# Perceiver block on one core: the opening loads of the context regrouped, the first batch's Gram sums in banks of their own, a new order of steps, and a shorter close

## What is computed

```python
# cross attention, 16 heads, no softmax: x = x + this(layernorm(x), ctx_1024, ctx_1024)
score = jnp.einsum('bhqd,bhkd->bhqk', Q, K) / dk
attn = jnp.where(mask, -jnp.inf, score)
ctx = jnp.einsum('bhqk,bhkd->bhqd', attn, V)
x = residual + _linear(ctx, wo_w, wo_b)          # then layer norm with ln_g, ln_b
# self attention, 64 tokens a batch, softmax: x = x + this(layernorm(x))
attn = jax.nn.softmax(scores, axis=-1)
# second self attention with rotary q and k, then the dense part: x = x + this(layernorm(x))
x = _rmsnorm(src + sa, norm1_w)
shared = _swiglu(flat @ W_shared_in) @ W_shared_out
h = _swiglu(flat @ W1_shared)
for e in range(E):                               # w: top 2 of the best group's 4 experts
    routed = routed + h @ W2_experts[e] * w[:, e:e + 1]
return _rmsnorm(x + shared + routed, norm2_w)
```

## Time and profile before

| | us |
|---|---|
| median of 3 runs (lowest, highest) | 263.49 (262.86, 266.23) |
| the profiled execution's own time | 262.64 |
| its span, first to last instruction | 260.5 |
| TensorE busy | 240.4 (92%) |
| VectorE busy | 174.3 (67%) |
| ScalarE busy | 121.0 (46%) |
| GpSimd busy | 75.9 (29%) |
| mean DMA rate | 101 GB/s |

### The profile page before, as it was taken

The page is one execution under the profiler, slowest core; times in us unless marked ns, Lnnn a source line. Parts: engine busy times, 40 slices in busy tenths (PEclk is TensorE's granted clock), DMA queues, the critical chain, the costliest instruction groups (busy, mean ns, idle before and its releaser), DMA issues.

```text
span 260.5 us, 5316 instructions
## 1 busy us (share of the span) xinstructions
PE 240.4 (92%) x2116; PEld 213.6 (82%) x2116; DVE 174.3 (67%) x366; ACT 121.0 (46%) x240; POOL 75.9 (29%) x87
## 2 busy tenths in 40 slices
PE   8678899999999999999998899999989999999980
PEld 8677899889988899997977789888768889988860
DVE  2537857797967787976855779656699652375345
ACT  4524752391443864667253495844661435530000
POOL 2001304372224303412334237467700011520003
PEclk9799999999999999999999999999999999999996
DMA  6997769566035034065202003150000000000002
GB/s 199 381 389 262 264 201 310 179 186 230 0 93 164 0 101 153 3 177 159 80 3 84 0 1 103 60 135 32 0 0 3 0 3 3 0 0 0 3 1 81
DMA packets 8856, 26.33 MB, mean 101 GB/s; under 512 B 1400, under 2 KB 3072, under 8 KB 8576
## 3 DMA queue, kind: packets, MB, share of 16 engines
q1 hardware_dynamic: 8832, 25.99, 30.6%
HBM read 25.46 MB, written 0.52 MB: 100 GB/s over the span
## 4 chain that ended last, share of the span: by engine, by line
PE 73%; DVE 9%; issue 5%; DMA 4%; ACT 3%; POOL 3%; SPq 1%; DVEq 0%; POOLq 0%; ACTq 0%
PE ps L677 68%; PE ps L680 5%; DMA raw<-in_ctx 4%; POOL rstd L441 2%; DVE qs L1221 1%; POOL dense L476 1%; DVE Z L1013 1%; ACT ch L552 1%; DVE st L990 1%; DVE Z L1262 1%; ACT kblk L501 1%; DVE X L1271 1%; SPq L383 1%; DVE Z L1001 1%; DVE cl L1110 0%
## 5 line engine op out<-in xcount | busy, mean ns | idle before, releaser
L677 PE MATMUL ps<-ch 128*128 128x130 f32 (+1 forms) x208 | 53.0, 271 | 3.8 <-DVE cl L1110 2.3
L677 PE MATMUL ps<-ch,cl 128*128 128x260 f32 (+1 forms) x208 | 53.4, 319 | 0.0
L677 PE MATMUL ps<-w,hT 128*128 128x512 f32 x192 | 46.5, 399 | 0.0
L441 POOL TENSOR_TENSOR rstd<-ve,half_exp 128x1 f32<-128x1 f32 (+1 forms) x22 | 13.6, 622 | 112.3 <-DVE ve L985 112.2
L677 PEld LDWEIGHTS ps<-ch 128*128 128x128 f32 (+1 forms) x208 | 41.6, 200 | 4.7 <-issue 2.8
L677 PEld LDWEIGHTS ps<-w,hT 128*128 128x128 f32 x192 | 35.7, 188 | 8.8 <-issue 0.3
L677 PEld LDWEIGHTS ps<-ch,cl 128*128 128x128 f32 (+1 forms) x208 | 41.3, 198 | 0.1
L1110 DVE TENSOR_TENSOR cl<-raw,ch 128x1024 fp32r<-128x1024 f32 (+1 forms) x23 | 32.9, 1433 | 10.5 <-ACT ch L552 9.8
L552 ACT ACTIVATE ch<-raw 128x1024 fp32r<-128x1024 f32 (+1 forms) x23 | 25.8, 1132 | 7.3 <-DMA raw<-in_ctx 6.8
L677 PE MATMUL ps<-xHL,dense 128*128 128x256 f32 x192 | 23.8, 284 | 0.0
L677 PEld LDWEIGHTS ps<-xHL,dense 128*128 128x128 f32 x192 | 23.1, 189 | 0.2
(11 more groups left out here) (161 smaller groups left out, 436.4 us busy)
## 6 DMA issues: line engine op xcount, KB each, us to landing
raw<-in_ctx SPq DMA_DIRECT2D x23, 512.0 KB, 4.8
raw<-in_w SPq DMA_DIRECT2D x8, 512.0 KB, 3.7
w<-in_w SPq DMA_DIRECT2D x2, 1024.0 KB, 7.1
stage<-in_dense SPq DMA_DIRECT2D x4, 512.0 KB, 5.3
mask<-in_mask SPq DMA_DIRECT2D x1, 800.5 KB, 10.4
rows<-in_rows SPq DMA_DIRECT2D x1, 768.0 KB, 7.8
raw<-in_ctx SPq DMA_DIRECT2D x8, 65.0 KB
raw<-in_ctx SPq DMA_DIRECT2D x4, 128.0 KB, 2.4
```

The source lines that it names most:

```text
L441: pool.tensor_tensor(rstd[:, lo:hi], ve[:, lo:hi], half_exp[:, lo:hi], ALU.pow).then_inc(sem("rstd"), 1)
L677: return pe.matmul(o, l, r, start=start, stop=stop, skip_group_check=not check)
```

## The change

- **Loads of chunks 0 and 1.** Chunk 0 is loaded as row 0 and rows 1 to 3 (it was four single rows) and still split row by row; chunk 1 is loaded and split in two halves (it was whole). `gram` 1 waits for each half.
- **Loads beside.** `w0` moves from after chunk 3 to after chunk 5, `rows` from after chunk 4 to after chunk 5, the mask from after chunk 6 to after chunk 7.
- **Banks.** Batch 0's sums go to `CROSS_B` (6, 7); batch 1 starts in `GRAM_B` with no wait for `g`.
- **Order.** All four parts of the list are new. The batches' norms, the attention steps, the dense products and the weight pieces stand in other places; `last_square` and `last_root` of tiles 0 and 1 and `finish` of tiles 0 to 2 stand before the last expert steps.
- **Close.** `last_root` multiplies Z by the weight row while POOL makes the root, and `finish` is one instruction. The last expert product is made as two halves of 256 columns in two banks.

```diff
-        ("gram", 0), ("gram", 1), ("gram", 2), ("split", 0), ("split", 1), ("split", 2), ("split", 3), ("split", 4),
-        ("norm0", 0), ("evac", 0), ("gram", 3), ("norm0_end", 0), ("gram", 4), ("cross1", 0), ("split", 5),
-        ("pre", 0), ("cross2_product", 0), ("qb", 0), ("flag", 0), ("norm0", 1), ("cross2", 0), ("gram", 5),
-        ("norm0_end", 1), ("split", 6), ("split", 7), ("evac", 1), ("cross3", 0), ("pre", 1), ("cross4", 0),
-        ("cross1", 1), ("gram", 6), ("split", 8), ("cross2_product", 1), ("split", 9), ("qb", 1), ("cross2", 1),
-        ("flags", 0), ("cross3", 1), ("masked", 0), ("gram", 7), ("cross4", 1), ("split", 10), ("gram", 8),
-        ("evac", 2),
+        ("split", 0), ("gram", 0), ("gram", 1), ("gram", 2), ("split", 1), ("split", 2), ("split", 3), ("split", 4),
+        ("norm0", 0), ("evac", 0), ("gram", 3), ("split", 5), ("norm0_end", 0), ("gram", 4), ("cross1", 0),
+        ("gram", 5), ("cross2_product", 0), ("evac", 1), ("split", 6), ("cross2", 0), ("pre", 0), ("cross3", 0),
+        ("cross4", 0), ("qb", 0), ("flag", 0), ("cross1", 1), ("gram", 6), ("split", 7), ("cross2_product", 1),
+        ("split", 8), ("cross2", 1), ("gram", 7), ("norm0", 1), ("gram", 8), ("split", 9), ("norm0_end", 1),
+        ("split", 10), ("cross3", 1), ("evac", 2), ("pre", 1), ("cross4", 1), ("cross1", 2), ("qb", 1), ("flags", 0),
+        ("masked", 0),
...
-        ("xo_product", 0), ("xo", 0), ("xo_end", 0), ("norm1", 0), ("norm1_end", 0), ("split", 11), ("cross1", 2),
-        ("gram", 9), ("gram", 10), ("turn_z", (0, 0)), ("proj1_product", 0), ("piece", 0), ("split", 12),
...
+        ("xo_product", 0), ("xo", 0), ("split", 11), ("gram", 9), ("xo_end", 0), ("cross2_product", 2), ("norm1", 0),
+        ("gram", 10), ("norm1_end", 0), ("split", 12), ("gram", 11), ("cross2", 2), ("turn_z", (0, 0)), ("split", 13),
...
-        ("cross2_product", 3), ("cross2", 3), ("split", 14), ("turn_p", (0, 0)), ("cross3", 3), ("values", (0, 0)),
-        ("cross4", 3), ("project", (0, 0)), ("norm2", 0), ("norm2_end", 0), ("xo_product", 1), ("xo", 1),
-        ("gram", 14), ("split", 15), ("xo_end", 1), ("split", 16), ("turn_z", (0, 1)), ("proj2_product", 0),
-        ("evac", 4), ("rotate", 0), ("keys2", 0), ("gram", 15), ("values2", 0), ("roped", 0),
+        ("turn_p", (0, 0)), ("cross3", 3), ("split", 15), ("values", (0, 0)), ("cross4", 3), ("project", (0, 0)),
+        ("gram", 14), ("norm2", 0), ("split", 16), ("evac", 4), ("xo_product", 1), ("norm2_end", 0), ("xo", 1),
+        ("split", 17), ("xo_end", 1), ("turn_z", (0, 1)), ("gram", 15),
...
-        ("norm1", 1), ("keys_roped", 0), ("cross1", 4), ("gram", 16), ("score_product", (0, 1)), ("norm1_end", 1),
-        ("piece", 2), ("turn_z", (1, 0)), ("score", (0, 1)), ("proj1_product", 1), ("split", 17), ("queries", 1),
...
+        ("norm1", 1), ("split", 18), ("proj2_product", 0), ("gram", 16), ("rotate", 0), ("keys2", 0), ("values2", 0),
+        ("roped", 0), ("keys_roped", 0), ("norm1_end", 1), ("gram", 17), ("cross1", 4), ("turn_z", (1, 0)),
+        ("score_product", (0, 1)), ("proj1_product", 1), ("score", (0, 1)), ("piece", 2), ("piece", 3), ("split", 19),
...
+        ("xo_product", 3), ("score", (2, 0)), ("piece", 6), ("piece", 7), ("exp", (2, 0)), ("hidden_product", 0),
+        ("hidden_product", 1), ("xo", 3), ("hidden", 0), ("hidden", 1), ("hidden_product", 2), ("hidden_product", 3),
+        ("shares", (2, 0)), ("hidden", 2), ("xo_end", 3), ("hidden_product", 4), ("hidden_product", 5),
+        ("turn_p", (2, 0)), ("norm1", 3), ("norm1_end", 3), ("piece", 8), ("gates", 0), ("hidden_product", 6),
...
-        ("experts_product", (3, 3)), ("experts", (3, 1)), ("experts", (3, 2)), ("last_square", 2),
-        ("experts", (3, 3)), ("last_root", 0), ("last_root", 1), ("last_square", 3), ("last_root", 2),
-        ("last_root", 3), ("finish", 0), ("finish", 1), ("finish", 2), ("finish", 3),
+        ("hidden_product", 8), ("experts", (1, 1)), ("experts", (1, 2)), ("last_root", 0), ("experts", (1, 3)),
+        ("hidden_product", 9), ("hidden_product", 10), ("hidden", 8), ("hidden_product", 11), ("hidden", 9),
...
+        ("last_root", 2), ("experts", (3, 1)), ("finish", 1), ("experts_product", (3, 3)), ("experts", (3, 2)),
+        ("experts", (3, 3)), ("last_square", 3), ("finish", 2), ("last_root", 3), ("finish", 3),
...
+    def expert_parts(use):
+
+        return [slice(0, D), slice(D, 2 * D)] if use == HALVES * USES - 1 else [slice(0, 2 * D)]
...
-        return [(r, r + 1) for r in range(ROWS)] if n == 0 else [(0, ROWS)]
+        return ([(r, r + 1) for r in range(ROWS)], [(0, 2), (2, ROWS)])[n] if n < 2 else [(0, ROWS)]
 
     def splits(n):
 
-        return ROWS + n
+        return ROWS + n + (n > 0)
+
+    def first_loads(eng, parts, n):
+
+        src = d_ctx[0, 0:CH_B * ROWS * P, :].rearrange("(p r) d -> p r d", r=CH_B * ROWS)
+        for lo, hi in parts:
+            eng.dma_start(raw[:, ROWS * n + lo:ROWS * n + hi, :],
+                          src[:, n * ROWS + lo:n * ROWS + hi, :]).then_inc(sem(f"first{n}{lo}"), 16)
...
-                3: [(w0[:, :, :, :], d_w0, "w0_in")],
-                4: [(X[:, :, :], d_x, "x_in"), (cols[:, :], d_cols, "cols_in"),
-                    (rows[:, :, :], d_rows.partition_broadcast(P), "rows_in")],
-                6: [(mask[:, :], d_mask, "mask_in")],
+                4: [(X[:, :, :], d_x, "x_in"), (cols[:, :], d_cols, "cols_in")],
+                5: [(w0[:, :, :, :], d_w0, "w0_in"), (rows[:, :, :], d_rows.partition_broadcast(P), "rows_in")],
+                7: [(mask[:, :], d_mask, "mask_in")],
...
-                for lo, hi in chunk_parts(n):
-                    sp.dma_start(raw[:, ROWS * c + lo:ROWS * c + hi, :],
-                                 src[:, c * ROWS + lo:c * ROWS + hi, :]).then_inc(sem(f"raw{c}" if n else f"first{lo}"), 16)
+                if n == 0:
+                    first_loads(sp, [(0, 1), (1, ROWS)], 0)
+                elif n == 1:
+                    first_loads(sp, chunk_parts(1), 1)
+                else:
+                    sp.dma_start(raw[:, ROWS * c:ROWS * c + ROWS, :],
+                                 src[:, c * ROWS:c * ROWS + ROWS, :]).then_inc(sem(f"raw{c}"), 16)
...
+                    banks = GRAM_B if i else CROSS_B
                     act.wait_ge(sem("gram_chunk"), CH_B * (i + 1))
                     if i >= 2:
                         act.wait_ge(sem("gs"), i - 1)
-                    copy(gab[:, i % 2, :, :, :].rearrange("p k c n -> p k (c n)"), ps[:, GRAM_B[0]:GRAM_B[1] + 1, 0:3 * GBLK], sem("g"))
+                    copy(gab[:, i % 2, :, :, :].rearrange("p k c n -> p k (c n)"), ps[:, banks[0]:banks[1] + 1, 0:3 * GBLK], sem("g"))
...
-                    if i:
+                    if i > 1:
                         pe.wait_ge(sem("high_done"), splits(i))
                         pe.wait_ge(sem("low_done"), splits(i))
-                    if b and c == 0:
+                    banks = GRAM_B if b else CROSS_B
+                    if b > 1 and c == 0:
                         pe.wait_ge(sem("g"), b)
                     for r in range(ROWS):
                         if i == 0:
                             pe.wait_ge(sem("high_done"), r + 1)
                             pe.wait_ge(sem("low_done"), r + 1)
-                        last = gram_tile(c, r, P, c == 0 and r == 0, False)
+                        elif i == 1 and r % 2 == 0:
+                            pe.wait_ge(sem("high_done"), ROWS + r // 2 + 1)
+                            pe.wait_ge(sem("low_done"), ROWS + r // 2 + 1)
+                        last = gram_tile(banks, c, r, P, c == 0 and r == 0, False)
                     if c == CH_B - 1:
-                        last = gram_tile(c, ROWS, TAIL, False, True)
+                        last = gram_tile(banks, c, ROWS, TAIL, False, True)
                     last.then_inc(sem("gram_chunk"), 1)
...
-                    split_products(
-                        ps[:, DENSE_B[use % 4], :],
-                        [([hT[:, 1, a, k, tok] for a in range(2)], [w2[:, u, a, k, :] for a in range(2)])
-                         for k in range(HID // P)]).then_inc(sem("products"), 1)
+                    for n, cols_ in enumerate(expert_parts(use)):
+                        if n:
+                            pe.wait_ge(sem("taken"), use - 2)
+                        split_products(
+                            ps[:, DENSE_B[(use + n) % 4], cols_],
+                            [([hT[:, 1, a, k, tok] for a in range(2)], [w2[:, u, a, k, cols_] for a in range(2)])
+                             for k in range(HID // P)]).then_inc(sem("products"), 1)
...
+                    if step == "last_root":
+                        link(dve.tensor_tensor(Z[:, i, :], Z[:, i, :], rows[:, 5, :], ALU.mult))
...
-                    link(rms_scaled(5, i, root_of["last_root", i]))
```

(4 more changed lines are left out.)

114 lines of the change are left out of this document (55 added, 59 removed), and 9 rows, old and new, of the table USES.

## The result

| | before | after |
|---|---|---|
| median, us (lowest, highest; runs) | 263.18 (261.84, 266.23; 4) | 254.25 (253.77, 255.43; 4) |
| the profiled execution's own time, span | 262.64, 260.5 | 253.77, 251.9 |
| TensorE busy | 240.4 | 236.8 |

What follows compares the result with a forecast made beforehand. TensorE, busy in 92% of the span, was taken as the bound. Gains of 3.1 (opening), 2.5 (middle) and 2.9 (close), 8.5 us off 262.64, gave 254.1, put at a median of 254.5; range 250.5 to 258.9.

Steps and rivals of the forecast that it cites:

- Opening, 3.1: Start to `cross1` 0: begins at 18.3 instead of 21.42, 3.1 us gained, bounds 1.0 to 4.4.
- At 391 GB/s the 0.2 MB less is 0.5 us: `w0` at 18.3: Opening's loads: `w0` lands at 18.3, with 5.22 MB in by its end instead of 5.42 MB by 18.85.
- rival (b): Opening gains only 1.0 to 1.5 us, `w0` late or the clock falling at the new wait; 256.3 in all, chance 0.13.
- Chunk 2's wait, 1.5: Ahead of `gram` 2: the wait for chunk 1 becomes one of some 1.5 us for chunk 2, with no clock drop.
- Middle, 2.5: Between `cross1` 0 and the close: fewer TensorE waits, 2.5 us gained, bounds 4.5 gained to 1.5 lost.
- 5.6 - 3.1: Middle: 5.6 us of listed TensorE waits removable, less 3.1 us of new waits the order makes.
- Close, 2.9: Last matmul to the span's end: 4.6 us instead of 7.5, 2.9 us gained, between 2.5 and 3.1.
- (a): Rival on the opening: early loads speed up, `w0` at 17.0, 1.3 us more gain, 253.2 in all; chance 0.12.
- (c): Rival on the middle: it gives nothing, DVE late as often as in the old order, 257.0; chance 0.10.
- (d): Rival on the attention steps: softmaxes lose their cover, slower; three uncovered ones, 19 us, give 273.6; chance 0.03.
- The prediction is wrong if `w0` lands after 20: Failure sign in the opening: `w0`, forecast at 18.3, landing after 20 us would show the prediction wrong.
- The estimate from the page: Opening's loads: fixed 2.0 us plus bytes at 436 GB/s puts the first three chunks in by some 6.5 us.

Runs made afterwards that it cites:

- the five other profiles: Profiled executions of five experiment kernels with the changed kernel's loads, banks and opening list; `cross1` 0 begins at 19.05 to 20.25 us in them.
- the run with fillers: The changed kernel with 18 more products of `blank`, result unused, on TensorE ahead of `gram` 2: 254.87 us, ratio 0.9644 to the kernel before.
- the two kernels with mixed lists: New loads, banks and close; one with only the new opening list, otherwise old order (263.88 us), one with the new first half's list too (259.84 us).
- the run in which POOL waits: The changed kernel with POOL's subtraction for weight piece 11 held until DVE has scaled tile 3's row: 251.87 us, ratio 0.956 to the kernel before.

## Why the prediction was right

The time was right to 0.25 us because two terms were off by about 2.4 each in opposite directions. The direction rests on steps that hold, and each of the three terms has the right sign. That the sum came out as forecast is luck.

- **Opening, 3.1: mis-sized. 0.7 to 0.8 in the pair of profiles, just below my lower bound of 1.0, and 1.8 by the mean of six.** The step that failed is "At 391 GB/s the 0.2 MB less is 0.5 us: `w0` at 18.3". It took the rate of a queue that is always full. The queue ran thin from 12 to 14 us (270 GB/s), with chunk 5's issue waiting for split 2 until 11.58, which stands in rival (b) as "the queue may run dry". The bound that I had named for this, 7.8 us from its own issue, is nearer: 8.1 here, 6.4 to 7.7 in the five other profiles, from issues at 12.1 to 12.8. The other half of rival (b), the clock, came true too and cost nothing (the run with fillers): the opening is bound by transfers, of which `w0` and chunk 5 are level.
- **Chunk 2's wait, 1.5: it was 2.5** (1.8 to 2.1 in three of the others). The delay within chunk 0 and the splitting of chunk 1 did what I said; I had `gram` 0 and 1 end near 10, and they ended by 9.2. It cost nothing for the same reason. The banks gained nothing that the times show. So "3.1" counted three effects, of which two could not reach the end where `w0` and chunk 5 were behind them.
- **What the loads are for I missed.** They are worth 3.2 us in the new order, of which 1.8 are seen in chunk 5, for a `gram` 5 that the new order wants early. The prediction looked only up to `cross1` 0.
- **Middle, 2.5: mis-sized, 5.0 measured, above my upper bound of 4.5.** My step was "5.6 - 3.1" from listed waits. The list after has 3.9 us besides the copies of `z0T` where I had 3.1, with one wait of 1.7 that I had not seen (POOL over DVE); in this the step held. What failed is the base: the removable loss was not 5.6 but more, because waits under 0.2 us, and as much of every longer one, are inside busy time. The 5.1 on the timeline's scale is no accident of one execution: from `cross1` 0 to the last matmul's end the profiles with the old banks and with the last product whole have 226.5 and 226.6 us too, where before had 231.7. The count shows 5.7 gained in 75 to 90 and 124 to 160 us, and the run with the old second half confirms that it is the order of these steps that makes it.
- **Close, 2.9: right.** 2.8 in the profile, 2.4 (1.6 to 3.2) by the run with the close alone. That the root, the square and one `finish` remain behind the last addition, and nothing queues, is in the rows of the end.
- **Rivals.** (a) falls: chunk 2 was split at the same time as before. (b) was the truth for the opening in the changed kernel's profile, with 0.7 to 0.8 where it had 1.0 to 1.5; its clock fell too, at no cost. (c) falls with 5.0 gained in the middle. (d) falls: no wait for `taken` and one of 0.2 us for the softmax's last step.
- **Signs.** "The prediction is wrong if `w0` lands after 20" came true (20.5), and the sum was saved by the middle; in four of the five other profiles `w0` landed before 20. A clock of 0.50 after 7 us and a wait of 2.5 ahead of `gram` 2 were against me too. No wait ahead of `gram` 3, and 4.75 from the last matmul to the end, were as I had said.
- **The estimate from the page.** The Trainium skill (DMA: Bandwidth & Descriptors, Anatomy of one DMA) gives the 2.0 us and 436 GB/s for transfers that GpSimd issues. These are issued by SP, and ACT took up chunk 2 at 8.76 after, where the estimate had it in by 6.5; to keep it out of the sum was right.

Open: how much of the loss of the two kernels with mixed lists is their seams alone, for which no list that mends one seam at a time was tried; which steps of the second half make its 3.8 us; and what the old order would take with the new loads but the mask in its old place. Nor was it tried to free chunk 5's slot earlier, which might let both `w0` and chunk 5 come forward.

## What to carry to other kernels

When transfers bound a stretch, find all that are level at its end before a gain is put down for one; here TensorE's clock and its wait for chunk 2 cost nothing in the opening, and moving `w0` forward cost 2 to 3 us. A list of waits is a lower bound of what an order can win: count from start times, since waits shorter than the modelled tail of a matmul don't show. And an order and its loads go together: on top of the new close the loads (with the banks) were worth nothing in the old order, the order 2.7 us with the old loads, and both together 5.9. Last, one profile is one execution: the opening of the same instructions ended anywhere from 19.05 to 20.59.

## What the hardware showed that I had not expected

VectorE and GpSimd can shut each other out for whole instructions. DVE's `TENSOR_SCALAR` 128x256 with both sides in SBUF took 2.44 us under a POOL subtraction of 2.36 and 0.41 without it, and POOL's own time stayed the same: the later one waited until the first had ended. It goes the other way too, on POOL's inverse root, which took 0.55 us alone and 1.48 us where a split of DVE had begun just ahead of it (from the run in which POOL waits):

```profile
73.48 1.23 DVE L1134 TENSOR_TENSOR cl<-raw,ch 128x1024 fp32r<-128x1024 f32 x1
```

```profile
73.64 1.48 POOL L454 TENSOR_TENSOR rstd<-ve,half_exp 128x1 f32<-128x1 f32 x1 [7.41 <-DVE ve L1009]
```

By the Trainium skill (SBUF — State Buffer, Who interferes with whom) the two engines share a pair of SBUF ports, which an instruction that uses it locks for its whole length, and whoever issues first has it; the trace agrees, with the numbers above. The profile puts such a wait down as busy time of the blocked engine, so it is found by comparing each instruction with the shortest of its kind.
